# Where GpSimd's powers of the state begin, and how finely VectorE's side work is cut

## The reference, cut to what matters

```
x = x + 0.5 * ffn(layernorm(x))
x = x + s4(layernorm(x))            # K from 32 states, causal convolution, gelu, @ W.T + b
x = x + 0.5 * ffn(layernorm(x))

ffn(x): h = silu(lin(x, w1)) * lin(x, w2)      # 256 -> 1024
        h = gelu(lin(h, h1)); h = gelu(lin(h, h2)); lin(h, w3)   # 1024 -> 1024 -> 1024 -> 256
s4:     dtA = A*dt;  C' = C*(exp(dtA)-1)/A;  K[d,l] = 2*Re(sum_n C'[d,n] * exp(dtA[d,n]*l)),  l < 1024
```

## Time and profile before

| | |
|---|---|
| median of 3 runs | 1349.6 us |
| the profiled execution | 1349.34 us |
| its span, first to last instruction | 1347.6 us |
| PE busy | 1317.4 us, 98% |
| DVE busy | 894.2 us, 66% |
| ACT busy | 746.4 us, 55% |
| POOL busy | 380.2 us, 28% |
| mean granted TensorE clock | 0.994 |

### The profile page before, as it was taken

One profiled execution on the slowest core, in us unless ns is written; L12 is line 12 of the kernel. 1 busy time (PEld: TensorE's weight loads), 2 busy tenths in 40 slices (PEclk: granted clock), 3 DMA queues, 4 the chain that ended last, 5 costly groups with the idle time before them and its releaser, 6 DMA issues.

```text
span 1347.6 us, 18334 instructions
## 1 busy us (share of the span) xinstructions
PE 1317.4 (98%) x7278; PEld 670.0 (50%) x7278; DVE 894.2 (66%) x1746; ACT 746.4 (55%) x1201; POOL 380.2 (28%) x350
## 2 busy tenths in 40 slices
PE   8999889999999999999999999999999999999997
PEld 3454344555544545455454554545545455454544
DVE  5266968842553786878778787787877873454723
ACT  5474435765446457474574745747457464445522
POOL 5811644200010352605326053260532500001000
PEclk9999989999999999999999999999999999999999
DMA  9210000000010000000000000000000001131400
GB/s 333 97 47 9 9 0 9 9 1 17 1 47 16 1 17 1 9 9 0 10 7 9 9 17 9 24 9 9 17 9 24 9 17 71 53 104 42 146 0 18
DMA packets 44701, 41.88 MB, mean 31 GB/s; under 512 B 32704, under 2 KB 41408, under 8 KB 41920
## 3 DMA queue, kind: packets, MB, share of 16 engines
q1 hardware_dynamic: 44608, 40.64, 10.2%
HBM read 28.57 MB, written 4.19 MB: 24 GB/s over the span
## 4 chain that ended last, share of the span: by engine, by line
PE 91%; DVE 5%; ACT 2%; DMA 1%; issue 0%; SPq 0%; DVEq 0%
PE psf L1335 62%; PE psf L1323 15%; PE psf L1347 8%; PE pss L1398 2%; PE pss L1408 2%; PE pss L1388 2%; DVE hab L623 1%; PE pss L1378 1%; DVE arena L582 1%; DVE arena L243 1%; ACT g L1146 1%; DMA g<-w 1%; PE pss L1363 0%; ACT hab L1100 0%; DVE arena L584 0%
## 5 line engine op out<-in xcount | busy, mean ns | idle before, releaser
L1335 PE MATMUL psf<-hab,wall 128*128 128x512 f16 x4096 | 890.8, 379 | 3.9 <-DVE ht L635 2.1
L1335 PEld LDWEIGHTS psf<-hab,wall 128*128 128x128 f16 x4096 | 399.3, 98 | 485.2 <-issue 6.4
L1107 ACT ACTIVATE psf<-psf,scf 128x512 f32<-128x512 f32 x256 | 168.6, 659 | 427.2 <-PE psf L1335 427.0
L623 DVE SCALAR_TENSOR_TENSOR hab<-psf,hab 128x512 f16<-128x512 f32 x256 | 175.1, 687 | 314.6 <-ACT hab L1100 314.3
L1323 PE MATMUL psf<-h,wall 128*128 128x512 f16 x1024 | 235.1, 383 | 16.0 <-DVE hab L623 13.0
L1323 PEld LDWEIGHTS psf<-h,wall 128*128 128x128 f16 x1024 | 99.7, 98 | 134.4 <-DVE hab L623 15.1
L1100 ACT ACTIVATE hab<-psf 128x512 f16<-128x512 f32 x256 | 152.9, 597 | 8.1
L972 POOL TENSOR_SCALAR rs<-mv 128x4 f32<-128x4 f32 x16 | 3.1, 194 | 507.9 <-DVE mv L666 502.0
L635 DVE SCALAR_TENSOR_TENSOR ht<-psf,scf,sil 128x512 f32<-128x512 f32 x128 | 95.1, 749 | 67.5 <-PE psf L1323 63.3
L1090 ACT ACTIVATE sil<-psf,scf 128x512 f32<-128x512 f32 x128 | 87.3, 686 | 92.3 <-PE psf L1323 90.6
L623 DVE SCALAR_TENSOR_TENSOR hab<-ht,hab 128x512 f16<-128x512 f32 x128 | 116.2, 914 | 3.3
(11 more groups left out here) (130 smaller groups left out, 912.2 us busy)
## 6 DMA issues: line engine op xcount, KB each, us to landing
arena<-wh SPq DMA_DIRECT2D x8, 1024.0 KB, 5.7
g<-wh SPq DMA_DIRECT2D x6, 1024.0 KB, 8.6
out<-xr SPq DMA_DIRECT2D x15, 256.0 KB, 2.2
xr<-x SPq DMA_DIRECT2D x7, 512.0 KB, 5.1
arena<-w SPq DMA_DIRECT2D x3, 1024.0 KB, 5.4
g<-w SPq DMA_DIRECT2D x2, 1024.0 KB, 6.8
xr<-wh SPq DMA_DIRECT2D x2, 1024.0 KB, 10.2
g<-w SPq DMA_DIRECT2D x2, 512.0 KB, 6.2
```

The costliest lines, as they stand in the source:

```text
L623: e.scalar_tensor_tensor(out=hab[:, buffer(p), m, 1, :], in0=source(p), scalar=2.0 ** E2 if l else 1.0, in1=hab[:, buffer(p), m, 0, :], op ...
L1107: e.activation(bank, bank, ACT.Gelu, scale=scf[:, 2 + l, m:m + 1]).then_inc(s_gelu, 1)
L1335: ins = e.matmul(bank[:, :], WH[:, l, m // 2, k, ms], hab[:, buffer(p), k, part, :], start=(k == 0 and part == 0), stop=(k == KH - 1 and p ...
```

## The change

The two quotas at the end of a layer, slots 14 and 15, fall from 1500 and 1000 to 1000 and 0. Passes 0 to 3 get a list of their own, with quotas 0 in the up slots as before, but 3000 in slot 25. The first step of an exponential is cut in two, and each step of the doubling too. GpSimd's strand zeroes its staging area as before, but then is held to the slot and the count of the factors (pj), no more of the state's powers (z). In the rates on GpSimd, cast(3) keeps its place behind the cut.

```diff
-BESIDE = [0, 500, 2000, 2700, 2700, 2700, 2000, 6800] + [0, 500, 2000, 2700, 2700, 2700, 1500, 1000]
+BESIDE = [0, 500, 2000, 2700, 2700, 2700, 2000, 6800] + [0, 500, 2000, 2700, 2700, 2700, 1000, 0]
 BESIDE += [200, 200, 200, 200, 1300, 200, 200, 1300, 200, 7300]
+
+TAPS_BESIDE = BESIDE[:16] + [0, 0, 0, 0, 1300, 0, 0, 1300, 0, 3000]
...
         self.two(a, a, 127.0, 0.0, ALU.min, ALU.add)
+        yield 3 * quick(src)
         self.two(c, a, -LN2_HI, 0.0, ALU.mult, ALU.add)
         self.add(b, c, src)
         self.two(c, a, -LN2_LO, 0.0, ALU.mult, ALU.add)
-        yield 5 * quick(src) + cost(src)
+        yield 2 * quick(src) + cost(src)
...
                         ch.done(ch.e.tensor_tensor(us[h], qf[side][h][:, :, 0:nr], zz[h ^ q], ALU.mult))
+                    yield 2 * cost(us[0])
                     ch.after()
                     ch.done(ch.e.tensor_tensor(qf[side][q][:, :, nr:2 * nr], us[0], us[1], op))
-                    yield 3 * cost(us[0])
-
+                    yield cost(us[0])
...
-                quota = (0 if s < 0 or i < FIRST - 1 and s in UPS else BESIDE[s]) - fixed(i, s)
+                quota = (0 if s < 0 else TAPS_BESIDE[s] if i < FIRST - 1 else BESIDE[s]) - fixed(i, s)
...
                 yield 4000
-                w.wait_ge(s_dve, mark["z"][1])
+                yield At(mark["pj"][0])
+                w.wait_ge(s_dve, mark["pj"][1])
...
             for n, _ in enumerate(rates(ch)):
-                if n == 3:
+                if n == 4:
                     cast(3)
```

## The result

The kernel after takes **1342.84 us** (median of 4 runs, 1341.33 to 1344.0), the one before 1349.61 beside it (4 runs, 1347.72 to 1351.54): a ratio of 0.9947, with an interval from 0.9935 to 0.9959. That is faster by 0.5%, more than the 0.3% that a measurement tells from no change, and 2.0 us over the forecast of 1340.8. The profiled execution took 1344.0 us, the slowest of its four, and its span fell by 5.4 us, from 1347.6.

A forecast was written before the change was run, and what follows sets the result against it. TensorE, busy 98% of the span, bounds the kernel; only its idle time can change. 17.3 us saved less 8.8 lost in pass 2 (1.0 + 6.0 + 1.8) gives 1349.34 - 8.5 = 1340.8 us, range 1332 to 1347.

The forecast's parts named there:

- a new wait of 4 to 11 us with the clock behind it: The forecast case: 4 to 11 us lost in pass 2, clock with it, 1336 to 1345 us; chance 0.57.
- What bounds the kernel: TensorE works 98% of the span; the change can only give back its idle time, some 30 us, or add to it.
- Pass 0, 1.9 saved: End of pass 0: exponential steps move to slots 20, 23, 25 with over 2 us of slack; TensorE's 1.91 us wait goes.
- Pass 1, 10.7 and 1.8 of the clock: End of pass 1: VectorE's factors run without GpSimd's large work beside them; the 10.7 us wait and 1.8 of clock go.
- the 0.6 behind them: TensorE's 0.61 us wait at 194 us, behind pass 1's long wait; claimed saved with it.
- GpSimd's new place: GpSimd starts about 160 us, idles about 170 to 195.7, then works beside pass 2's slots 3 to 14 until 248.
- The layer's border, 1.0: Pass 2, slots 3 to 6 beside GpSimd: slot 7's low half comes late, a wait of 1.0 us (0 to 8.9).
- Slots 11 to 13, 6.0: Pass 2: VectorE's doubling beside GpSimd makes slot 14's low half late, a new wait of 6.0 us (0 to 10).
- The clock, 1.8: Behind pass 2's new wait: slow clock costs 1.8 us, as after the 10.7 wait; 0 if the clock holds.
- the first: Rival 1: no new wait in pass 2 (under 4 us, no clock loss); 1332 to 1336, say 1334 us; chance 0.25.
- The second and third: Rivals: pass 2 loses 13.3 to 21.4 us, no change, about 1347, chance 0.12; or 22.5, slower, 1354.5, chance 0.06.
- the rule of the Trainium skill: VectorE and GpSimd lock their shared port pair for whole instructions; slots 12 and 13 cost 2.8 us more, wait near 9.

The follow-up runs named there:

- experiment 6: experiment 3 with slot 23 of pass 0 left empty and a quota of 4300 in slot 25 for what it held; 1331.8 us.
- experiment 1: The kernel before, with only GpSimd held to the factors, quotas and whole steps as before; 1346.04 us, ratio 0.9965 to the kernel before.
- experiment 2: The kernel after without GpSimd's hold to the factors, cuts and quotas kept; 1344.76 us, ratio 0.9963 to the kernel before.
- experiment 7: The kernel before with only GpSimd's hold and its late round 1, cuts and quotas as before; 1339.52 us, ratio 0.9924 to the kernel before.
- experiment 4: The kernel after with the factors' mark naming slot 14, where the last factor step is issued, instead of slot 23; 1338.5 us.
- experiment 3: The kernel after with GpSimd's round 1 doubling waiting until TensorE has read the last product of its round 0 (slot 14); 1333.05 us.
- experiment 9: experiment 4 with slot 23 left empty in passes 0 and 1, and 4300 in slot 25 of pass 0; 1331.59 us.

## Why the prediction was right, and where its sizes were off

The prediction was right in sign and range, and its forecast, a new wait of 4 to 11 us with the clock behind it, is what came. The forecast time is 2.0 us under the median. Compared with the profiled execution, from which it was reckoned, it is 3.2 us too low: 8.5 us were to be gained, and 5.3 were (1349.34 to 1344.0). By its steps:

- **What bounds the kernel.** Right. TensorE's idle time is what changed, and the span followed it: pass 3 starts at 275.23 for 280.97, 5.74 earlier, and the span is 5.4 shorter. Nothing moved from pass 5 on that can be told from noise: the two waits on VectorE there are 0.38 and 0.59 before, 0.39 and 0.60 after.
- **Pass 0, 1.9 saved.** This step failed: the claim of over 2 us of slack for the work of slots 20, 23 and 25. Slot 23 had under 1 us. The wait of 1.91 at the end of pass 0 came back as 1.25 at the start of pass 1, so that 0.7 was saved in place of 1.9. TensorE begins a layer with three tiles and asks for the three banks, the third of which is free only with the gate that VectorE's slot 23 holds up. In VectorE's timeline after, the slot's three instructions stand straight ahead of that gate:

```profile
101.53 0.62 DVE L257 TENSOR_SCALAR arena<-arena 128x896 f32<-128x896 f32 x1
102.19 1.09 DVE L253 TENSOR_TENSOR arena<-arena 128x896 f32<-128x896 f32 x1
103.32 0.63 DVE L257 TENSOR_SCALAR arena<-arena 128x896 f32<-128x896 f32 x1
103.86 1.40 DVE L638 SCALAR_TENSOR_TENSOR ht<-psf,scf,sil 128x512 f32<-128x512 f32 x2
```

  The first of the two gates ends near 104.6 and the layer starts at 104.86; without these three it starts with no wait (experiment 6, where that gate ends at 103.2 and the layer starts at 103.99, 0.8 later). I had named the banks, but counted the slack only to the last input tile (36 matmuls). The slots 20 and 25 did have the slack.
- **Pass 1, 10.7 and 1.8 of the clock.** Right, in full, and for the reason given (experiments 1 and 2). Of the 0.6 behind them 0.36 stayed. Pass 2 so starts 13.35 earlier, not 15.0: 1.3 from pass 0, 0.3 from here.
- **GpSimd's new place.** Right in its order, late by 1 to 5 us: start 161.03 for 160, idle from 172 to 197.3 for 170 to 195.7, round 0 done at 220.8 for 216, the doubling of round 1 at 244.7 for 241, its halves at 252.7 for 248. The 4 to 5 us come in two parts. Round 0 goes on at 199.31, behind the layernorm's scales, where it had been set in line from 197. And GpSimd's own instructions are slower beside VectorE too: the rest of round 0 took 21.5 for 19, of it the halves 3.36 + 5.63 = 9.0, where they had taken 7.1 before (2.02 + 5.08, at 165.86 and 167.84).
- **The layer's border, 1.0.** It did not come. The last low half of the input (slot 7) ran at 216.20 and ended 0.7 later, so by 216.9, while the need had moved from 216.5 to 218.1, as pass 2 began 1.7 us later than forecast. Experiments 1 and 7 show that the estimate was of the right kind: with the old cuts and quotas the same place costs 1.96 and 1.94.
- **Slots 11 to 13, 6.0.** It was 6.90. The forecast had 20.5 us from 230.4, to 250.9. It was 22.2, from 231.58 to 253.8, and the need was at 247.0, not 245.1. (The prediction's own parts, 5.8 and some 0.5 for slot 15, had given 6.3; the latter did not come.) The doubling's rates held on the whole (pairs 2.87 and 2.35 for 2.98, thirds 1.64 and 2.49 for 1.64): slot 11 took 7.0 for 7.3, slot 12 5.4 for 5.8. What was mis-sized is slot 13, 7.3 for 5.3, above all its cast: taken at 0.65, its time alone, it took 2.42 beside GpSimd. No run took the cast away; by the sum it is 1.8 of the 2.0.
- **The clock, 1.8.** It was 3.1, a miss of 1.3, as large as that of pass 0: the loss behind the wait of 10.7 did not carry over to one of 6.9. The clock is low for about as long in both (roughly 167.2 to 177.5 before, 249.6 to 259.8 after, estimated from the granted clock of slices of 1 and 2 us), but the shorter wait leaves TensorE more of that time to work in: 3.4 us (from 174.14) before, 5.9 (from 253.87) after. At half the clock half of it is lost, 1.7 and 3.0.
- **The sum.** 8.5, less 1.3 and 0.4 in passes 0 and 1, plus 1.0 at the border, less 0.9 and 1.3 in pass 2, is 5.6, and the profiled executions differ by 5.3. The medians differ by 6.8. The misses do not cancel by much, only the border's 1.0 hides a part of the others: that the time came out in the range rests on the mechanism, not on luck.

Of the rivals, the first (no new wait) counts on small sizes beside VectorE's slots and on large steps that miss each other. They did not miss each other, and the window from 200 to 252 after has GpSimd busy for 49.39 of its 52 us. The second and third wanted 13.3 us and more in pass 2, and it was 10.0.

On the rule of the Trainium skill (SBUF — State Buffer, section "SBUF: two separate sides"): by it the wait would have been near 9, and it was 6.9; for the doubling's pairs the trace's own rates were the better guide. Experiment 4 agrees with the rule in kind all the same: VectorE's small instructions end with GpSimd's large ones, which is a wait for a whole instruction. How often the two meet had to come from the trace.

## What to carry to other kernels

A stall that comes from two engines in each other's way is not removed by moving one of them to where it meets the other again: ask where the moved work will run and what runs there, work off both streams, and put the large pieces of the one beside a stretch in which the other has only small or fixed work, as experiment 3 does and experiment 9 for the most part. Keep short side steps out of the last slots ahead of a start that asks for several buffers together: in experiment 4 each of them cost one of the neighbour's instructions, however small it was. And look at the clock behind every wait of a few microseconds: here it added from a sixth to three quarters of the wait again.

## What the runs showed of the hardware

- The price beside GpSimd is by the instruction: 0.92 and 1.23 us for 128x16, which takes 0.19 alone (experiment 4), where a difference of 128x512 goes from 0.69 to between 1.42 and 2.49 (kernel after).
- Operations with one input are held up too: a cast of 128x1024 took 2.42 us for 0.69 in slots with the same order (kernel after, experiment 3), and two took 4.52 at 216.81 in the kernel after. The low halves that read the PSUM tile (psf) stayed at 0.68 in all of this; those that read SBUF alone (from ht) rose to 2.60 in experiment 4.
- The slow clock needs no single long wait. In experiment 1 it fell to 0.50 near 251, behind a wait of 1.44 us and within one of 1.56, and stayed there through the next two; in experiment 7 it fell at 273.0, behind one of 2.20, when TensorE had been back at work for 1.2 us:

```profile
250.00:252.00 2.00, 0.44 (x2) 0.13 (x2) 1.97 (x7) 0.00 (x0) 0.00 (x0) 0.73 0.00 0
252.00:260.00 8.00, 5.44 (x13) 1.47 (x12) 7.78 (x16) 1.43 (x3) 0.00 (x0) 0.50 0.00 0
```

  These two lines are of experiment 1, the granted clock third from the end.
- What it costs does not grow with the wait: 1.7 us behind 2.20, 1.4 behind 4.68, 3.1 behind 6.90, 1.8 behind 10.70. It is half of the time that TensorE works at 0.50, in the same order: 3.4 us (273.0 to 276.4, experiment 7), 2.8 (185.59 to 188.4, experiment 4), 5.9 and 3.4 (as above). When the level falls and rises again stays open; no run varied the wait by itself.
